# Transposes of the identity in TensorE's first waits, and the first small loads on SyncE's queue

## The reference

```python
def _L0_ffn_ref(x, Win, bin_, W1, b1, W2, b2, Wout, bout):
    s = jnp.einsum('btd,dm->btm', x, Win) + bin_
    h = jax.nn.relu(s[..., None] * W1 + b1)
    g = jnp.einsum('btmh,mh->btm', h, W2) + b2
    out = jnp.einsum('btm,md->btd', g, Wout) + bout
    return out
x = L0_attn_x
xn = _layernorm(x, axis=-1)
x = x + _L0_attn_ref(xn, ...) + _L0_ffn_ref(xn, ...)
```

## Time and profile before

| | before |
|---|---|
| median of 3 runs | 328.38 us (328.0 to 328.88) |
| the profiled execution | 329.03 us |
| its span, first to last instruction | 327.2 us |
| TensorE busy | 90% of the span |
| DVE busy | 79% |
| ScalarE and GpSimd busy | 72% each |

### The profile page before, as it was taken

How to read it: one execution, slowest core, us unless ns; L and a number is a source line. 1 busy time by engine, 2 the same in 40 slices (tenths; PEclk the granted TensorE clock), 3 DMA queues, 4 the chain that set the end, 5 groups by cost and what they waited for, 6 DMA issues and landing times.

```text
span 327.2 us, 5159 instructions
## 1 busy us (share of the span) xinstructions
PE 296.1 (90%) x1804; PEld 132.0 (40%) x1804; DVE 257.5 (79%) x400; ACT 234.0 (72%) x308; POOL 237.0 (72%) x209
## 2 busy tenths in 40 slices
PE   3797499989989999999999999999999999999683
PEld 3543364544433544344443434343434243432220
DVE  1818965589599787897879999989897989976435
ACT  1516755675896869879698668888878788886830
POOL 8523992771992989659892966978969496989930
PEclk9999989999999999999999999999999999999999
DMA  7999929995529899698979999899999997425458
GB/s 237 300 373 405 256 23 337 403 212 193 182 94 331 230 310 317 180 343 248 334 198 314 314 297 310 249 351 270 332 309 354 334 373 245 184 115 219 134 184 339
DMA packets 50569, 87.80 MB, mean 268 GB/s; under 512 B 6360, under 2 KB 35184, under 8 KB 46448
## 3 DMA queue, kind: packets, MB, share of 16 engines
q1 hardware_dynamic: 46400, 65.96, 66.1%
q10 hardware_dynamic: 3504, 21.37, 18.0%
q0 software_dynamic: 640, 0.16, 0.8%
HBM read 53.77 MB, written 33.69 MB: 267 GB/s over the span
## 4 chain that ended last, share of the span: by engine, by line
PE 60%; DVE 25%; DMA 6%; issue 5%; ACT 2%; SPq 0%; ACTq 0%; DVEq 0%
PE op L548 13%; PE s L489 13%; PE g L526 12%; PE T L465 7%; DVE stats L957 6%; DVE x L930 6%; PE rep L510 3%; DMA out_dram<-x 3%; DMA x<-in_L_attn_x_dram 3%; PE op L347 2%; DVE xqT L940 2%; ACT H L701 1%; PE A L320 1%; DVE SL L951 1%; PE A L418 1%
## 5 line engine op out<-in xcount | busy, mean ns | idle before, releaser
L1064 POOL TENSOR_TENSOR x<-x,bias_row 128x512 f32<-128x512 f32 x128 | 162.7, 1313 | 2.5 <-DVE bias_row L812 2.5
L701 ACT ACTIVATE H<-rep,b1c,w1c 128x1024 f32<-128x1024 f32 x128 | 146.8, 1220 | 17.7 <-PE rep L510 13.2
L930 DVE TENSOR_TENSOR x<-x,op 128x1024 f32<-128x1024 f32 x62 | 75.1, 1211 | 29.0 <-PE op L548 28.9
L957 DVE BATCH_NORM_STATS2 stats<-x 128x6 f32<-128x512 f32 x128 | 80.7, 678 | 7.8 <-DMA x<-in_L_attn_x_dram 7.6
L548 PE MATMUL op<-wout,G 64*128 64x512 f32 x248 | 68.4, 628 | 5.2 <-DVE x L930 5.2
L1048 POOL TENSOR_TENSOR rstd<-veps,nhalf 128x8 f32<-128x8 f32 x16 | 26.7, 1671 | 51.7 <-DVE veps L967 51.6
L526 PE MATMUL g<-H,w2s 128*32 128x512 f32 x512 | 63.0, 600 | 0.4 <-ACT H L701 0.4
L489 PE MATMUL s<-xT,win 128*64 128x512 f32 x128 | 59.9, 612 | 0.9 <-ACT xqT L676 0.8
L676 ACT ACTIVATE xT<-T 128x512 f32<-128x512 f32 x60 | 36.4, 606 | 31.0 <-PE T L465 27.3
L489 PE MATMUL s<-xqT,winq 128*64 128x512 f32 x112 | 51.1, 598 | 0.0
L465 PE MATMUL T<-ident,x 128*128 128x128 f32 x256 | 43.5, 295 | 6.0 <-ACT xT L676 2.9
(11 more groups left out here) (170 smaller groups left out, 291.3 us busy)
## 6 DMA issues: line engine op xcount, KB each, us to landing
out_dram<-x SPq DMA_DIRECT2D x30, 1024.0 KB, 6.1
x<-in_L_attn_x_dram ACTq DMA_DIRECT2D x10, 2048.0 KB, 11.8
xq<-in_L_attn_x_dram SPq DMA_DIRECT2D x112, 128.0 KB, 7.3
x<-in_L_attn_x_dram SPq DMA_DIRECT2D x12, 1024.0 KB, 11.5
out_dram<-x SPq DMA_DIRECT2D x4, 512.0 KB, 3.3
x<-in_L_attn_Wq_dram SPq DMA_DIRECT2D x1, 1024.0 KB, 17.6
x<-in_L_attn_Wk_dram SPq DMA_DIRECT2D x1, 1024.0 KB, 19.8
x<-in_L_attn_Wv_dram SPq DMA_DIRECT2D x1, 1024.0 KB, 17.2
```

Of the source, the lines that this page charges most:

```text
L701: act.activation(Hr[half][k % len(Hr[half])][:, :], rep_ps[:, :], ACT.Relu, bias=b1c[:, half, k:k + 1], scale=w1c[:, half, k:k + 1]).then_ ...
L930: dve.tensor_tensor(both, both, sum_banks(n, j)[:, :].rearrange("p (h d) -> p h d", h=2), ALU.add).then_inc(add_done, 1)
L957: dve.bn_stats(stats[:, j, :], x_sb[m][:, j * D:(j + 1) * D]).then_inc(bn_done, 1)
L1064: pool.tensor_tensor(x_sb[m][:, c], x_sb[m][:, c], bias_row[:, :], ALU.add).then_inc(xc_done, 1)
```

## The change

TensorE gets a function `keep_busy(count)`: `count` transposes of the identity, with the identity itself as both operands, into `o_ps`, which nothing reads. Nothing waits for them and they wait for nothing. Eight stand in front of body 0, behind the attention's first step, and 18 in body 0 between parts 1 and 2 of the transposes. The nine loads at the start of ScalarE's queue move to SyncE's: those of `xa` and `lna` behind `load(1, 0)`, those of `winq` behind `load(1, 1)`. DVE's statistics of `xa` move from -32 to 13, which is behind the variance of body 0.

```diff
--- before.py
+++ after.py
@@ -196,7 +196,7 @@
             46, 46, 65, 65, 65, 69, 69, 71, 72, 72, 72, 104, 104, 106, 108, 128, 128, 132, 138, 142, 163, 164, 165,
             167, 170, 170, 192, 200, 206, 227, 228, 229, 231, 234, 234, 256, 264, 270, 290, 296,))
         AT_DVE = iter((
-            -32, -32, -32, 34, 36, 40, 41, 41, 41, 41, 48, 48, 48, 64, 69, 69, 73, 77, 77, 77, 80, 96, 98, 100, 102,
+            -32, -32, 13, 34, 36, 40, 41, 41, 41, 41, 48, 48, 48, 64, 69, 69, 73, 77, 77, 77, 80, 96, 98, 100, 102,
             130, 130, 134, 135, 140, 141, 161, 192, 193, 194, 195, 200, 201, 225, 256, 257, 258, 259, 264, 265, 289,
             290, 292,))
         AT_POOL = iter((
@@ -272,7 +272,12 @@
             load(0, 0)
             load(0, 1)
             load(1, 0)
+            for b in range(B):
+                sp.dma_start(xa[b * LT:(b + 1) * LT, :], x[b, 0:LT, :]).then_inc(in_xa, 16)
+            sp.dma_start(lna, lna_w.partition_broadcast(RW)).then_inc(in_lna, 16)
             load(1, 1)
+            for i in range(DC):
+                sp.dma_start(winq[i * QD:(i + 1) * QD, :, :], Win.rearrange("(i j b) m -> i b j m", i=DC, b=QD)[i, :, :, :]).then_inc(in_winq, 16)
             sp.dma_start(bias_row[:, :], bout.partition_broadcast(P)).then_inc(in_rows, 16)
             sp.dma_start(row1, bo.partition_broadcast(P)).then_inc(in_rows, 16)
             load_weight(0, Wq)
@@ -549,10 +554,16 @@
                                start=True, stop=True, tile_position=(b * M, 0))
             mm.then_inc(op_done, 1)
 
+        def keep_busy(count):
+
+            for _ in range(count):
+                pe.transpose(o_ps[:, 0:P], ident[:, :], ident[:, :])
+
         def pe_program():
             pe.wait_ge(ident_made, 1)
             side = [-PLACES, pe_attention()]
             reach(side, -1, 0)
+            keep_busy(8)
             for n in range(BODIES):
                 if has(n):
                     transpose(n, 0)
@@ -575,6 +586,8 @@
                 if has(n - 2):
                     sum_h(n - 2, 0)
                 reach(side, n, 6)
+                if n == 0:
+                    keep_busy(18)
                 if has(n):
                     transpose(n, 2)
                 reach(side, n, 7)
@@ -708,11 +721,6 @@
             act.activation(G[n % 2][:, :].rearrange("m (j p) -> m j p", j=TILES), g_ps[:, :].rearrange("m (p j) -> m j p", j=TILES), ACT.Identity, bias=b2c[:, 0:1]).then_inc(g_made, 1)
 
         def act_program():
-            for b in range(B):
-                act.dma_start(xa[b * LT:(b + 1) * LT, :], x[b, 0:LT, :]).then_inc(in_xa, 16)
-            act.dma_start(lna, lna_w.partition_broadcast(RW)).then_inc(in_lna, 16)
-            for i in range(DC):
-                act.dma_start(winq[i * QD:(i + 1) * QD, :, :], Win.rearrange("(i j b) m -> i b j m", i=DC, b=QD)[i, :, :, :]).then_inc(in_winq, 16)
             side = [-PLACES, act_attention()]
             reach(side, -1, 0)
             for n in range(BODIES):
```

## The result

The changed kernel takes 330.89 us, median of 20 runs (328.44 to 333.83), against 327.47 (325.52 to 329.22) for the kernel before in runs taken in turn with it. The ratio is 1.0075, 95% interval 1.0051 to 1.0100: slower by some 2.5 us, where 2.2 us of gain were predicted. The ratio leaves out two slow executions of the changed kernel (333.38 and 333.83), while the medians, which take in all 20, are 3.4 us apart. 326.2 was forecast, the range ended at 328.1.

What follows compares the result with a forecast made beforehand. TensorE was taken as the bound before 25 us and in the long middle, DVE between 25 and 40. Terms 0 + 0 + 0 - 2.2 from the 328.38 us median gave 326.2 us, range 324.4 to 328.1.

Steps and rivals of the forecast that it cites:

- What bounds the kernel: Whole span: TensorE busy 90%, so each microsecond cut from the start lets the steady TensorE work begin earlier.
- The transposes: Body 0's start: 26 identity transposes raise TensorE's clock at 9.5 us, so the input product ends at 19.5; gain 2.2 us.
- rival (a): Start: the clock doesn't rise in time and the transposes are plain extra work, 3.0 us later, 331.4 us; chance 0.10.
- at most that 1 us: Start: x's second half may land up to 1 us sooner, worth at most that; counted as 0.
- The moved loads: Nine loads from ScalarE's to SyncE's queue: later SyncE issues and body 3's load stay covered; cost 0.
- the issues replace waiting: SyncE's queue: nine issues, 4.6 us, fall into some 12 us of hold-up already there; cost 0.
- all add: SyncE's queue: if all 4.6 us came on top, body 3's load would be issued at 50.4, costing up to 3.5 us.
- Its transfers were not waited for in it: DVE's stretch from 25.33 to 40.27 us: moves up by 2.2 us as it is, without waits for transfers.
- (d): After the start: the lead is lost to transfers, a store or body 3's load, giving 328.4 us; chance 0.13.
- DVE's statistics: Statistics of xa, 0.68 us, moved behind the first body's variance, fit into DVE's 6.34 us of idle; cost 0.
- The second low stretch: Clock at 0.50 from 40.3 to 43.6 us, costing 1.6 us: taken as before, 0; ends 1.6 gained or 1.5 lost.

Runs made afterwards that it cites:

- e1: Kernel before plus only the 26 transposes of the identity, the nine loads staying on ScalarE's queue: 328.38 us, ratio 1.0023.
- e12: Changed kernel with SyncE's 13 small parameter loads moved behind body 3's x and quads: 329.82 us, ratio 1.0048.
- e2b: Second profile of the kernel before with only the nine loads moved and DVE's step at 13, no transposes: 333.27 us; that kernel's ratio 1.0106.
- e13: Kernel before with only SyncE's 13 small parameter loads moved behind body 3's x and quads: 327.49 us, ratio 0.9990.
- e6: Kernel before plus 26 transposes of a 32x32 corner of the identity in TensorE's wait at the very start: 329.08 us, ratio 1.0033.
- e5: Kernel before plus 1 and 3 long products of the identity in place of the 8 and 18 transposes, loads not moved: 327.07 us, ratio 0.9985.
- e10: Kernel before with long identity products at the start, three near 37 us, one in each of two waits near 301 and 303 us: 325.85 us, ratio 0.9942.
- e9: Kernel before with long identity products at the start, three more near 37 us and four near 304 us: 328.81 us, ratio 1.0027.
- e3: Changed kernel with the four pieces of winq back at the start of ScalarE's queue: ratio 1.0019.

## Why the prediction was wrong, by its steps

**What bounds the kernel: right.** Where no transfer took it the start's lead went through: in e1 2.9 us at the start, 2.2 from 68 us on, behind the longer low stretch of the clock, and 2.96 at the last add, since before's own execution loses 0.7 at a store near 245 us.

**The transposes: the forecast times came, but not shown as their doing.** In after the gain at the scaling of s is 2.87 us for the 2.2 of the sum. The rise came at 9.56 as taken, which the prediction had chosen between two ends; in e12, with the same program, it came within the 18, so part of the agreement is luck. The difference in after lies in the joints: the 18 began at 10.03, not at 10.4, and the next transposes of x 1.96 us behind, since the last of the 18 overlaps them; so the product begins at 15.20, not at 15.9. The rival (a), that transposes bring no rise in time, fell for after and e1: the full clock came with nothing but transposes on TensorE since 5 us. The Trainium skill, "TensorE: Matmul & The Clock Gate", Part 4 (PE-mode transpose), says that the full clock doesn't engage for transposes; here the measurement decides, and it is against the page (groups of four at 1.06 before 9.5 us, at 0.63 from 9.56 on). What the step lacked is the other way to the same lead. It held that x's second half landing sooner is worth "at most that 1 us"; with the loads moved and no transposes of the identity the scaling of s was 3.35 and 3.49 us earlier, so in the changed kernel nothing shows a gain by the transposes.

**The moved loads, "Cost 0 in the sum": this is the step that failed.** The loads alone give 1.0106 (3.5 us), the transposes alone 1.0023. The reasoning was that SyncE is held up anyway, so "the issues replace waiting". The hold-up comes from the transfers in front of it, and so waiting is replaced only if they proceed as fast. They didn't: 230 and 277 GB/s for 297 and 357. SyncE was held in Wk's issue from 10.49 to 17.3 with the DMA engines at a share of 0.81, and everything behind was 3.7 us late, near the 4.6 that the step had worked out for issues that "all add". It was also priced at the wrong consumer. The step followed body 3's load, which is covered until 58; the piece that came late was the first group of quads, issued right behind. The prediction had said of them only "Its transfers were not waited for in it", with nothing on how far they were from being waited for. They cost 1.75 us in the profile of after; in that of e2b a wait of 5 us, and 2.9 more by the low clock behind it. How the 3.5 us divide over all executions isn't known. (d) named the effect, the lead lost to transfers, with 0.13 of the chance, and set its price to the lead at most (328.4), while a late load can take more than the lead: e2b lost 7.8 us against a lead of 3.5.

Why SyncE's queue feeds the engines worse with xa and lna in it is not settled. Winq's small packets alone don't do it. The number of issues remains as a cause: the nine take 5.4 us and put Wq and Wk, 2 MB, 5 us later into the queue. Placing the same nine behind Wk would tell, and was not done.

**DVE's statistics: right.** The wait of 3.95 us for xa lies in idle time, 1.69 us of it were left.

**The second low stretch: "as before, 0" was not a constant.** It is 3.4 us long in one profile of the kernel before and over 6 in the other. And it isn't independent of the loads: the second stretch of e2b followed TensorE's wait for the late quads.

**What was not in the sum at all: the end.** Six of the eight kernels that have the 52 instructions show a fetch of instructions within the last stores, at +1.3 us in after and +1.7 in e1, against before.

**What stays open.** The profiles of e1 and before differ by -2.96 + 1.75 = -1.2 us, as the two causes say; the means of all their runs differ by +0.5 (328.43 and 327.95 in this comparison). The 1.7 us between is where the two profiled executions lie in their own spreads, 0.7 below e1's mean and 1.0 above before's. So the start's 2.9 us are shown against executions of before with a late rise, and how much of them holds against its mean isn't; e13 suggests less. The times of e6 and e5 don't help: e6, with 52 instructions more, is at 1.0033 and e5, with 16, at 0.9985, though e6 leads at the scaling of s (22.34 against 23.96) and has no slow end in its profile. Why the transfers thin is open, by the number of issues or by what xa and lna are, and so is how much of the mean loss is wait, clock and end.

## What to carry to other kernels

When loads are moved to another queue, look not only at the next big load behind them but at every transfer that is issued from then on, and note how long each lay ready before its first reader: one that isn't waited for in the trace of before may have half a microsecond to spare. Such a wait can cost more than its length, when the clock falls behind it. Short work put into a wait pays if it is shorter than the wait (e10 against e9); each extra instruction is also code to be fetched, so few wide ones may be better than many narrow (e5 at 0.9985, e1 at 1.0023, with overlapping intervals). And with 1.2 us between executions of one kernel, a pair of traces can show less than a third of the difference, as here: where a wait looks small, profile a slower execution as well. The same holds for gains: profile the kernel before more than once, and each part of the change alone, before a lead is put down to one of them.

## What was not expected of the hardware

- Where one packet of 16 KB of instructions falls among the last stores, they end with over a microsecond at 18 to 29 GB/s (after, e1): 5.1 to 6.1 us from the last add to the end instead of 3.8 to 3.9 (4.7 in e3).
- TensorE's first rise to the full clock moves by several microseconds from one execution to the next: by 19.83, 18.08 and 16.05 in three executions with the same TensorE program and the same loads, at 9.56 in after and after 10.92 in e12. With 26 transposes of 32x32 at 1.6 us it came by 11.82, across waits of 1.39 and 1.22 us.
- A wait of TensorE for late transfers is followed by the low clock in one profile (idle 5.27 us, product 6.54 us instead of 3.65 in e2b) and not in two others (idle 2.27 and 1.84 us).
- The granted clock falls to 0.50 not only near 40 us but in some executions near 307, in the last bodies, at 2.3 to 2.4 us each time; matmuls of the identity in the waits ahead of the two places lifted its mean over the runs from 0.984 to 0.996 (e10).
- Nine small loads early in SyncE's queue (0.13 MB each of xa, lna and winq) go with 0.74 MB less moved between 10 and 20 us.
